# GpSimd adds the second layer norm's bias to each pair of expert tiles; the gates of the first stage are made at pair 8

## The chip, the cores and the metric

One of the eight cores of a Trainium2 chip runs the whole program. The metric is the device time of that core in microseconds (us). A run with a profile gives the span from the first to the last instruction, and its own time beside it.

## The reference

The input is x of 8 sequences with 256 tokens of 128 numbers, 2048 tokens, float32. Three residual steps follow each other: half of a mixture of experts, differential attention, and half of the same mixture again.

```
def ffn(x):                                   # per token, x is a layer-normed row
    p = softmax(x @ Wr + br)                  # 8 experts
    probs, idx = top_k(p, 2); probs /= probs.sum()
    h = layernorm(relu(x @ W1[e] + b1[e])) * g1[e] + be1[e]      # 128 -> 512
    y = layernorm(relu(h @ W2[e] + b2[e])) * g2[e] + be2[e]      # 512 -> 128
    return sum over the two chosen experts of gate[e] * y[e]
x = x + 0.5 * ffn(layernorm(x))
x = x + attention(layernorm(x))               # 8 heads, causal, lam = exp(lq1.lk1) - exp(lq2.lk2) + const
x = x + 0.5 * ffn(layernorm(x))
```

be2 is the bias that the change is about. Because it is added inside y[e], a token's output holds the sum of its two gates times its two rows of be2.

## The kernel before, in words

Only the two experts that a token chose are computed. The 4096 (token, expert) rows are sorted by expert into 39 tiles of 128 slots (`SLOT_TILES`), and the tiles go through the experts in 20 pairs (`PAIRS`); a tile has one expert, whose number each engine reads from the tile `eid` into a register (`experts`, L58). There are three stages: "f1" (first mixture), "at" (attention) and "f2" (second mixture). The order of the work on each engine is written out by hand, and semaphores join the engines.

**A pair in f1.** GpSimd gathers the rows of the pair's tiles from DRAM with an indirect DMA for each tile (`gather`, L517; `gather_pair(p)`, L535, fetches the tiles of pair p + 4 as soon as TensorE has turned those of pair p + 2). TensorE turns the rows (`turn_x`, L969), makes the hidden layer (`hidden`, L980), turns it (`turn_h`, L989) and makes the second product (`second`, L999). ScalarE empties PSUM (`copy_xT` L751, `relu` L758, `copy_hT` L764), makes square roots (L768, L772) and the last scaling (`finish`, L779), which writes the tile `yo` and counts the semaphore `yf`. VectorE makes the statistics (L1388 to L1419), adds the shifted bias b2 (L1407) and multiplies by g2 (`y_norm`, L1431). SyncE stores `yo` to the DRAM tensor y_scratch (L381) and, after every second pair, empties a part of another one (L428). In `body(n)` TensorE does turn_h(n), turn_x(n + 2), hidden(n + 1), second(n).

**Pairs 0 and 1** are written out, pairs 2 to 7 are a loop, and pairs 8 to 19 (`BESIDE` is 8) have work of the stages behind them woven in, by the functions `between(m)` and `behind(m)` of each engine with m = n - 8. For m = 0 to 3 TensorE and VectorE add the bias be2; from m = 3 on the y rows of sequences 0 and 1 are weighed and summed (`early_combine`, L2099) and their attention begins: statistics (L2109 to L2117), the root on GpSimd (`root`, L563), the norm (L2122). The y rows come by GpSimd's gathers (`token_rows`, L583), which wait for the stores of the pairs that they read.

**The bias be2 in f1.** The gates of the two choices are made ahead of pair 0: ScalarE takes the exponent of the logits' difference (L819), VectorE makes the gates (`gate_pairs`, L1271) and spreads them to a table of 8 experts for each token (`gate_sums`, L1277); TensorE turns this table (`turn_gates`, L1052), ScalarE copies it (L826). ScalarE also spreads be2 into the tile `be2x` with 16 copies (`own_bias`, L723). Four products of 128x512 (`shared_bias`, L1115) then give gates times be2 for all tokens, in pairs 8 to 11, and VectorE adds them to x (`add_bias`, L1459). The second mixture does the same at its end, with the same `be2x`. Beside the gates ScalarE and VectorE make lambda of the attention (L821, L1212, L1213).

**Around it.** `center_weights` (L2398) on VectorE comes behind the gates. On GpSimd `bias_rows` (L587) makes three rows from the router's bias for the second mixture, behind the last gather of f1. The attention (`att_gpsimd`, `att_scalar`, `att_tensor`, `att_vector`) begins with GpSimd's gathers of the y rows of sequences 2 and 3 (L1638), which wait for all y stores, and then runs in turns t = 2 to 9; each turn has on ScalarE `turned_half` (L945), the exponents (L1736), and `half_values` (L1715).

Of the kernel before, what the change touches and what calls it, by code (L numbers as in the profile page):

```python
# [21 lines left out]
P = 128  # L22
# [86 lines left out]
def build(nc, x, Wq, Wk, Wv, Wo, lq1, lk1, lq2, lk2, Wr, br, W1, b1, g1, be1, W2, b2, g2, be2, out, stages=("f1", "at", "f2")):  # L109
    with ExitStack() as ctx:  # L110
# [37 lines left out]
        be2x = sb("be2x", [P, TT, DIM])  # L148
        gmix = sb("gmix", [P, TOPK, TT, NE])
# [221 lines left out]
        def moe_sync(sp, S, first):  # L371
# [95 lines left out]
        def moe_gpsimd(pool, S, first):  # L467
# [71 lines left out]

            for p in range(BESIDE + 2):  # L540
                gather_pair(p)
            pool.wait_ge(S["gsum"], 1)
# [9 lines left out]
            gather_pair(BESIDE + 5)  # L552
            gather_rows(pool, 1, (1,))
            gather_pair(BESIDE + 6)
            gather_pair(BESIDE + 7)
            root(pool, 1)
            pool.tensor_scalar(picks[:, 0, 0, :], lo_iota[:, 0:NE], float(TT), None, ALU.mult).then_inc(F["base"], 1)
# [226 lines left out]
        def moe_scalar(act, S, first):  # L784
# [3 lines left out]
            if first:  # L788
# [39 lines left out]
            if first:  # L828
                gates_turned()
# [47 lines left out]
            if first:  # L877
# [127 lines left out]
        def moe_tensor(pe, S, first):  # L1005
# [50 lines left out]
            if first:  # L1056
                turn_gates()
# [17 lines left out]
            def between(m):  # L1075

                if m < 4:
                    shared_bias(m)
                if m == 4:
                    pe.wait_ge(s_ld_a, 80)  # L1080
                    pe.wait_ge(S["be2a"], 4)
                    turn_weights(pe, BESIDE_BANK)
# [28 lines left out]
            def shared_bias(q):  # L1111
                if first and q:
                    pe.wait_ge(S["be2a"], q)
                at = BESIDE_BANK if first else bank[BE2_BANKS[q]][:]
# [7 lines left out]
            if first:  # L1122
                turn_x(0, 0, 0)
                own_products(0)
                e = experts(pe, eid, 0, 6)
                pe.wait_ge(s_colc, 2 + NE)
# [310 lines left out]
        def expert_loop_vector(dve, S, step, first, steps):  # L1437
# [24 lines left out]
            def between(m):  # L1462

                if m < 4:
                    add_bias(m)
# [1097 lines left out]
```

## Time and profile before

| | us |
|---|---|
| runs of the kernel | 440.73, 441.86, 444.21 (median 441.86) |
| profiled execution, its own time | 438.17 |
| its span | 436.2 |
| TensorE busy | 385.0 |
| VectorE busy | 349.7 |
| ScalarE busy | 289.7 |
| GpSimd busy | 246.5 |

PE is TensorE's matmul, PEld its weight load, DVE is VectorE, ACT ScalarE, POOL GpSimd, SP SyncE. Times inside the profile count from the start of the span. A row of a timeline has start, duration, engine, line, operation and tiles; in brackets stands how long the engine was idle before it and what let it go. "issue" is time in which an engine waited for nothing that the profile shows. Matmuls overlap, so in the chain of waits a product counts 0.86 us where the timeline has 1.02 for the two of it.

### The profile page before, as it was taken

How to read it: one execution, taken by the hardware profiler on the slowest of the kernel's cores; microseconds unless marked ns; L12 is line 12 of the kernel's file. 1: busy time of each engine (PE TensorE's matmuls, PEld its weight loads, DVE VectorE, ACT ScalarE, POOL GpSimd, SP SyncE). 2: the span in 40 equal slices, each digit the busy share in tenths (PEclk: the TensorE clock that was granted, in tenths of full speed). 3: DMA queues.
4: the chain of work that ended last, by engine and by line, in shares of the span. 5: the costliest groups of instructions: out<-in, count | busy, mean ns of one | idle time of the engine just before them, and what ended most of it. 6: DMA issues, size and time to landing. Idle time of an engine off the chain costs nothing.

```text
span 436.2 us, 11622 instructions
## 1 busy us (share of the span) xinstructions
PE 385.0 (88%) x3570; PEld 271.8 (62%) x3574; DVE 349.7 (80%) x1302; ACT 289.7 (66%) x595; POOL 246.5 (57%) x343
## 2 busy tenths in 40 slices
PE   7887999999999868889898899887899899999864
PEld 7643577877777554556465565654577588787623
DVE  8895678887989797787888898867598788878864
ACT  3196787655777787778676778765665476776630
POOL 8786554346462056567574847568615767655530
PEclk9997999999999969999999999999999899999997
DMA  6930014654345311001000001011121222111036
GB/s 194 329 141 25 26 50 152 206 177 157 118 144 181 106 38 30 23 14 26 20 20 22 14 26 32 20 38 50 51 51 38 75 62 63 57 55 43 32 104 216
DMA packets 27444, 35.15 MB, mean 81 GB/s; under 512 B 4329, under 2 KB 20641, under 8 KB 26242
## 3 DMA queue, kind: packets, MB, share of 16 engines
q1 hardware_dynamic: 22450, 24.62, 17.3%
q0 software_dynamic: 4944, 9.90, 8.3%
q8 instruction: 27, 0.44, 0.4%
q14 instruction: 23, 0.19, 0.1%
HBM read 15.45 MB, written 18.24 MB: 77 GB/s over the span
## 4 chain that ended last, share of the span: by engine, by line
PE 50%; DVE 16%; POOL 12%; issue 8%; DMA 7%; ACT 4%; SPq 1%; DVEq 0%; POOLq 0%; ACTq 0%
PE bank L980 12%; PE bank L999 12%; PE bank L989 6%; DVE mx L2162 4%; POOL xr_scratch L463 3%; POOL orr L1669 2%; PE bank L1188 2%; DMA early<-y_scratch 2%; POOL yk L583 2%; DMA yk<-y_scratch,posi 2%; PE bank L969 2%; PE bank L2525 1%; PE bank L1925 1%; PE bank L1943 1%; PE bank L1183 1%
## 5 line engine op out<-in xcount | busy, mean ns | idle before, releaser
L999 PEld LDWEIGHTS bank<-w2c,hT 128*128 128x128 f32 x624 | 76.3, 194 | 21.8 <-issue 20.8
L999 PE MATMUL bank<-w2c,hT 128*128 x624 | 78.0, 279 | 3.5 <-ACT hT L764 3.4
L980 PE MATMUL bank<-w1s,xT 128*128 x156 | 74.1, 596 | 0.1
L2162 DVE TENSOR_REDUCE mx<-bank 128x4 f32<-128x1024 f32 (+1 forms) x48 | 58.4, 1220 | 8.6 <-PE bank L1885 8.6
L1736 ACT ACTIVATE early<-bank 128x768 f32<-128x768 f32 x64 | 51.8, 813 | 20.2 <-PE bank L1933 19.5
L1388 DVE BATCH_NORM_STATS2 st<-wide 128x6 f32<-128x512 f32 x78 | 50.0, 682 | 15.2 <-ACT wide L758 15.1
L764 ACT COPY hT<-bank 128x1024 f32<-128x1024 f32 (+1 forms) x40 | 39.5, 989 | 33.6 <-PE bank L989 33.6
L517 POOL DMA_INDIRECT xgw<-xn_scratch,slot_u x39 | 37.4, 958 | 34.1 <-PE bank L969 25.1
L487 POOL DMA_INDIRECT y_scratch<-yo,dest_u x39 | 38.9, 999 | 30.4 <-PE bank L989 16.0
L583 POOL DMA_INDIRECT yk<-y_scratch,posi x32 | 32.4, 1013 | 36.4 <-DMA y_scratch<-yo 14.4
L758 ACT ACTIVATE wide<-bank 128x1024 f32<-128x1024 f32 (+1 forms) x40 | 40.1, 1002 | 11.9 <-PE bank L980 11.1
L463 POOL DMA_INDIRECT xr_scratch<-row_buf,hi_i x32 | 31.8, 994 | 22.6 <-PE bank L1933 12.9
L989 PE MATMUL bank<-ident,wide 128*128 128x128 f32 x312 | 40.8, 273 | 0.0
L980 PEld LDWEIGHTS bank<-w1s,xT 128*128 128x128 f32 x156 | 27.0, 190 | 21.3 <-issue 21.0
L989 PEld LDWEIGHTS bank<-ident,wide 128*128 128x128 f32 x312 | 35.4, 142 | 0.8 <-issue 0.3
L945 ACT COPY wide<-bank 128x1024 bf16<-128x1024 bf16 x28 | 28.4, 1015 | 2.1 <-PE bank L1188 2.0
L1407 DVE SCALAR_TENSOR_TENSOR yy<-bank,r,b2p 128x128 f32<-128x128 f32 x78 | 24.6, 351 | 6.1 <-DVE r L1401 1.6
L779 ACT ACTIVATE yo<-yz,r 128x128 f32<-128x128 f32 x78 | 27.1, 397 | 3.3 <-DVE yz L1431 2.1
L1925 PE MATMUL bank<-mxT,sel 64*128 64x384 bf16 x128 | 21.5, 333 | 6.4 <-ACT early L1736 4.1
L1876 PE MATMUL bank<-mrhs,mlhs 64*128 64x128 bf16 (+1 forms) x192 | 15.6, 242 | 12.0 <-DVE mx L2162 9.2
L1431 DVE SCALAR_TENSOR_TENSOR yz<-yy,mv,g2b 128x128 f32<-128x128 f32 x78 | 23.4, 339 | 0.0
L563 POOL TENSOR_TENSOR ars<-ave,neg_half 128x2 f32<-128x2 f32 x8 | 5.8, 719 | 29.6 <-DVE ave L2117 29.6
(382 smaller groups left out, 880.2 us busy)
## 6 DMA issues: line engine op xcount, KB each, us to landing
xr_scratch<-row_buf SPq DMA_DIRECT2D x8, 1032.0 KB
xgw<-xr_scratch SPq DMA_DIRECT2D x39, 64.5 KB, 1.8
y_scratch<-yo SPq DMA_DIRECT2D x19, 128.0 KB, 1.9
w1s<-in_L_ffn_W_dram SPq DMA_DIRECT2D x1, 2048.0 KB, 8.9
early<-y_scratch SPq DMA_DIRECT2D x8, 256.0 KB, 4.0
xs<-in_L_attn_x_dram SPq DMA_DIRECT2D x4, 256.0 KB, 3.8
xn_scratch<-row_buf SPq DMA_DIRECT2D x1, 1024.0 KB
out_dram<-xs SPq DMA_DIRECT2D x8, 128.0 KB, 2.4
```

Of the source, the lines that this page charges most:

```text
L463: pool.indirect_dma_start(out=xr_dram, out_offset=bass.IndirectOffsetOnAxis(ap=slot2[:, c:c + 1], axis=0), in_=rows_of[t // HALF][:, t % H ...
L487: pool.indirect_dma_start(out=y_dram, out_offset=bass.IndirectOffsetOnAxis(ap=dest_u[:, 2 * p + j:2 * p + j + 1], axis=0), in_=yo[:, p % 2 ...
L517: pool.indirect_dma_start(out=xg[:, u, :], out_offset=None, in_=xn_dram, in_offset=bass.IndirectOffsetOnAxis(ap=slot_u[:, n:n + 1], axis=0 ...
L583: pool.indirect_dma_start(out=yk4[:, t % (2 * YRING), k, :], out_offset=None, in_=done, in_offset=bass.IndirectOffsetOnAxis(ap=posi[:, c:c ...
L758: act.activation(hh[:, u, 0:k, :], banks[:, h_at[u]:h_at[u] + k, :], ACT.Relu).then_inc(S["relu"], 1)
L764: act.copy(hT[:, u, 0:k, :], banks[:, 5:5 + k, :]).then_inc(S["hTc"], 1)
L980: last = pe.matmul(bank[h_at[u] + j][:], xT[:, u, j, :], w1s[:, bass.ds(e * FF, FF)], start=True, stop=True)
L989: last = pe.transpose(bank[5 + j][:, c * P:c * P + P], hh[:, u, j, c * P:(c + 1) * P], ident[:])
L999: last = pe.matmul(o[:, j * DIM:(j + 1) * DIM], hT[:, u, j, c * P:(c + 1) * P], w2c[:, bass.ds(e * (FC * DIM) + c * DIM, DIM)], start=(c = ...
L1388: last = dve.bn_stats(st1[:, u, j, :], hh[:, u, j, :])
L1736: act.activation(prob[:, g], quad[:, low:low + 2, 0:3 * P], ACT.Exp).then_inc(A["prob"], 1)
L2162: dve.tensor_reduce(mx[:, c:c + 2 * per].rearrange("p (a q) -> p q a", q=2), quad[:, low:low + 2, :].rearrange("p q (a e) -> p q a e", a=p ...
```

## The change

GpSimd adds be2 of the tile's expert to each row of `yo`, right behind ScalarE's last scaling, from a tile `be2b` that holds be2 of all experts on all partitions (loaded by one more broadcast DMA of 512 KB; it lies in the first half of `be2x`). SyncE's store waits for GpSimd's add (semaphore `be2`) in place of `yf`. With that, the first mixture's four bias products, their additions, the table of gate sums, its turn and its copy are gone. Both exponents become powers of e on GpSimd, behind the first gathers; VectorE makes the gates and lambda in pair 8. The adds stand one pair of gathers behind: `after_gather(p)` adds to pair p - 2. `bias_rows` and the second root come later in GpSimd's order. ScalarE's 16 copies into `be2x` move to the ends of the attention's turns 2 to 5, four each.

```diff
+        be2b = be2x[:].rearrange("p t d -> p (t d)")[:, 0:NE * DIM]
@@ moe_sync
-                    sp.wait_ge(S["yf"], p + 1)
+                    sp.wait_ge(S["be2"], p + 1)
@@ moe_gpsimd
+            def add_rows(p, es):
+
+                pool.wait_ge(S["yf"], p + 1)
+                for j in tiles[p]:
+                    last = pool.tensor_tensor(yo[:, p % 2, j, :], yo[:, p % 2, j, :], be2b[:, bass.ds(es[j] * DIM, DIM)], ALU.add)
+                last.then_inc(S["be2"], 1)
+
+            def after_gather(p):
+
+                at = (p - 2) % 4
+                if at == 0:
+                    after_gather.es = experts(pool, eid, 2 * p - 4, min(PACK, SLOT_TILES - 2 * p + 4))
+                add_rows(p - 2, after_gather.es[2 * at:])
+
+            pool.wait_ge(S["eid"], 1)
+            pool.wait_ge(s_bc, 32)
             for p in range(BESIDE + 2):
                 gather_pair(p)
+                if p == 0:
+                    pool.wait_ge(S["top"], 1)
+                    pool.tensor_tensor(gden[:], euler[:], mw[:], ALU.pow).then_inc(S["gexp"], 1)
+                if p == 1:
+                    pool.wait_ge(A["lam"], 1)
+                    pool.tensor_tensor(lam_e[:], euler[:, 0:2], lam_s[:], ALU.pow).then_inc(A["lame"], 1)
+                if p >= 2:
+                    after_gather(p)
             pool.wait_ge(S["gsum"], 1)
             pool.wait_ge(S["yst0"], 8 * BESIDE)
             pool.wait_ge(S["yst1"], 8 * BESIDE)
             gather_rows(pool, 0, (0,))
             gather_pair(BESIDE + 2)
+            after_gather(BESIDE + 2)
             gather_rows(pool, 0, (1,))
             gather_pair(BESIDE + 3)
+            after_gather(BESIDE + 3)
             root(pool, 0)
             gather_pair(BESIDE + 4)
+            after_gather(BESIDE + 4)
...
             gather_pair(BESIDE + 7)
+            after_gather(BESIDE + 7)
+            pool.tensor_scalar(picks[:, 0, 0, :], lo_iota[:, 0:NE], float(TT), None, ALU.mult).then_inc(F["base"], 1)
+            after_gather(BESIDE + 8)
             root(pool, 1)
-            pool.tensor_scalar(picks[:, 0, 0, :], lo_iota[:, 0:NE], float(TT), None, ALU.mult).then_inc(F["base"], 1)
+            for p in range(BESIDE + 9, PAIRS + 2):
+                after_gather(p)
             bias_rows(pool)
@@ moe_scalar, ahead of pair 0, and in pairs 0 and 1
-                act.wait_ge(S["top"], 1)
-                act.activation(gden[:], mw[:], ACT.Exp).then_inc(S["gexp"], 1)
-                act.wait_ge(A["lam"], 1)
-                act.activation(lam_e[:], lam_s[:], ACT.Exp).then_inc(A["lame"], 1)
-                act.activation(spad, eps_c[:], ACT.Sqrt)
-            if first:
-                gates_turned()
-                own_bias(act, 0, 4)
-                own_bias(act, 4, 10)
-                own_bias(act, 10, 16)
@@ moe_tensor
-            if first:
-                turn_gates()
-                if m < 4:
-                    shared_bias(m)
-                pe.wait_ge(S["gTc"], 1)
-            pe.wait_ge(s_be2x, 3)
@@ moe_vector and expert_loop_vector
-                gates(dve, S, step)
-                dve.wait_ge(A["lame"], 1)
-                step(dve.tensor_tensor(neg_lam[:], lam_e[:, 1:2], lam_e[:, 0:1], ALU.subtract))
-                step(dve.tensor_scalar(neg_lam[:], neg_lam[:], -LAMBDA_INIT, None, ALU.add))
             def between(m):
-                if m < 4:
-                    add_bias(m)
+                if m == 0:
+                    gate_pairs(dve, S, step)
+                    lambda_difference(dve, step)
+                    dve.memset(hold[:, 0:1], 0.0).then_inc(S["gsum"], 1)
@@ att_scalar, the end of a turn
+                if t == 2:
+                    act.wait_ge(sems["f1"]["be2"], PAIRS)
+                if 2 <= t < 2 + TT // BIAS_STEP:
+                    own_bias(act, BIAS_STEP * (t - 2), BIAS_STEP * (t - 1))
@@ center_weights and the prologue of gpsimd
-            dve.wait_ge(s_bc, 16)
+            dve.wait_ge(s_bc, 32)
+            pool.dma_start(be2b, be2.rearrange("(o a) d -> o (a d)", o=1).to_broadcast([P, NE * DIM])).then_inc(s_bc, 16)
```

`BIAS_STEP` is 4. TensorE's wait for the finished W1 (`s_colc`) moves ahead of the turn of pair 0.

## Rows read from the trace of the kernel before

**Rows 1.** The page, busy time of each engine, us and share of the span.
```profile
PE 385.0 (88%) x3570; PEld 271.8 (62%) x3574; DVE 349.7 (80%) x1302; ACT 289.7 (66%) x595; POOL 246.5 (57%) x343
```
**Rows 2.** Busy time by stretch; columns: stretch, length, PE, PEld, DVE, ACT, POOL, clock, DMA, GB/s.
```profile
58.60:81.80 23.20, 23.20 (x153) 18.17 (x152) 19.09 (x86) 17.63 (x40) 9.51 (x11) 1.00 0.44 150
...
86.40:108.20 21.80, 21.80 (x130) 16.06 (x129) 17.40 (x73) 13.06 (x28) 11.60 (x12) 1.00 0.49 163
108.20:129.60 21.40, 20.55 (x132) 15.91 (x132) 18.72 (x86) 15.57 (x38) 11.31 (x12) 1.00 0.43 139
129.60:149.00 19.40, 17.28 (x133) 13.64 (x132) 17.42 (x82) 15.04 (x32) 3.49 (x13) 1.00 0.40 137
```
**Rows 3.** Timeline ahead of pair 0, all engines.
```profile
38.30 0.97 POOL L517 DMA_INDIRECT xgw<-xn_scratch,slot_u  x1 [0.30 <-issue]
...
39.59 1.02 PE L2416 MATMUL bank<-early,yz 128*32 128x512 f32 x2
39.84 1.28 ACT L819 ACT_TABLE_LOAD   x1
...
43.47 0.38 PE L969 MATMUL bank<-ident,xgw 128*128 128x128 f32 x2
```
**Rows 4.** Row gathers (L517) from 36 to 50 us.
```profile
DMA to landing us min/median/max: 2.5/2.6/2.8
```
**Rows 5.** GpSimd's timeline in pairs 9 to 17.
```profile
93.40 0.94 POOL L517 DMA_INDIRECT xgw<-xn_scratch,slot_u  x1 [3.24 <-PE bank L969]
...
97.23 0.94 POOL L583 DMA_INDIRECT yk<-y_scratch,posi  x1 [1.64 <-DMA y_scratch<-yo]
...
113.75 0.74 POOL L563 TENSOR_TENSOR ars<-ave,neg_half 128x2 f32<-128x2 f32 x1 [6.59 <-DVE ave L2117]
...
138.12 0.71 POOL L563 TENSOR_TENSOR ars<-ave,neg_half 128x2 f32<-128x2 f32 x1 [8.46 <-DVE ave L2117]
...
142.26 0.20 POOL L599 TENSOR_TENSOR picked<-picked 128x8 bf16<-128x8 bf16 x1
```
**Rows 6.** The chain of waits in pairs 8 to 17; columns: start, duration, what.
```profile
87.68 0.86 PE bank L1115 x2
...
127.37 4.41 DMA xgw<-xn_scratch,slot_u
...
132.22 1.98 PE bank L980 x4
```
**Rows 7.** GpSimd's groups by shape; after the bar: busy us, mean ns.
```profile
L1633 POOL TENSOR_SCALAR row_buf<-xs,mv,rstd 128x128 f32<-128x128 f32 x12 | 10.1, 849 | 0.7
...
L1613 POOL TENSOR_TENSOR ysum<-yk 128x256 f32<-128x256 f32 x5 | 3.6, 715 | 0.0
...
L510 POOL TENSOR_TENSOR gden<-euler,mw 128x16 f32<-128x16 f32 x1 | 2.9, 2942 | 0.0
...
L2487 POOL DMA_DIRECT2D g2b<-in_L_ffn_g_dram x1 | 0.5, 533 | 0.0
...
L2363 POOL TENSOR_TENSOR b1lo<-early,b1hi 32x128 f32<-32x128 f32 x1 | 0.4, 421 | 0.1
```
**Rows 8.** Timeline behind the last pair.
```profile
152.47 0.40 ACT L779 ACTIVATE yo<-yz,r 128x128 f32<-128x128 f32 x1
...
155.26 1.32 POOL L583 DMA_INDIRECT yk<-y_scratch,posi  x1 [12.80 <-DMA y_scratch<-yo]
...
162.22 1.14 DVE L2099 SCALAR_TENSOR_TENSOR xs<-yk,gate,xs 128x128 f32<-128x128 f32 x4 [0.23 <-DMA yk<-y_scratch,posi]
```
**Rows 9.** ScalarE's spread of the bias, its first call.
```profile
49.80 1.27 ACT L725 ACTIVATE be2x<-be2p,own_t 128x128 f32<-128x128 f32 x4
```
**Rows 10.** ScalarE's timeline at the end of the attention's turn 2.
```profile
177.42 1.01 ACT L945 COPY wide<-bank 128x1024 bf16<-128x1024 bf16 x1
178.94 0.59 ACT L1715 COPY turned_o<-bank 128x512 f32<-128x512 f32 x1 [0.51 <-PE bank L1947]
```
**Rows 11.** VectorE's addition L2193, eight times; ns min/median/max.
```profile
L2193 DVE TENSOR_TENSOR od<-ow x8: 416/453/1298, 184.2 to 316.8; 128x256 f32<-128x256 f32 x8
```

More of the change, by code:

```diff
@@ L546, in moe_gpsimd @@
             gather_pair(BESIDE + 2)
+            after_gather(BESIDE + 2)
             gather_rows(pool, 0, (1,))
             gather_pair(BESIDE + 3)
+            after_gather(BESIDE + 3)
             root(pool, 0)
             gather_pair(BESIDE + 4)
+            after_gather(BESIDE + 4)
             gather_rows(pool, 1, (0,))
             gather_pair(BESIDE + 5)
+            after_gather(BESIDE + 5)
             gather_rows(pool, 1, (1,))
             gather_pair(BESIDE + 6)
+            after_gather(BESIDE + 6)
             gather_pair(BESIDE + 7)
+            after_gather(BESIDE + 7)
+            pool.tensor_scalar(picks[:, 0, 0, :], lo_iota[:, 0:NE], float(TT), None, ALU.mult).then_inc(F["base"], 1)
+            after_gather(BESIDE + 8)
             root(pool, 1)
-            pool.tensor_scalar(picks[:, 0, 0, :], lo_iota[:, 0:NE], float(TT), None, ALU.mult).then_inc(F["base"], 1)
+            for p in range(BESIDE + 9, PAIRS + 2):
+                after_gather(p)
             bias_rows(pool)
@@ L1111, in shared_bias @@
             def shared_bias(q):
-                if first and q:
-                    pe.wait_ge(S["be2a"], q)
-                at = BESIDE_BANK if first else bank[BE2_BANKS[q]][:]
+                at = bank[BE2_BANKS[q]][:]
                 pe.matmul(at, gsT[:], be2x[:, 4 * q:4 * q + 4, :], start=True, stop=True).then_inc(S["be2"], 1)
@@ L1122, in moe_tensor @@
             if first:
+                pe.wait_ge(s_colc, 2 + NE)
                 turn_x(0, 0, 0)
@@ L1125, in moe_tensor @@
                 e = experts(pe, eid, 0, 6)
-                pe.wait_ge(s_colc, 2 + NE)
                 hidden(0, 0, e[0:2])
@@ L1152, in moe_tensor @@
                 return
+            pe.wait_ge(s_be2x, TT // BIAS_STEP)
             e = experts(pe, eid, 2 * PAIRS - 8, 7)
@@ L1165, in build @@
         BE2_BANKS = (0, 1, 2, 4)
+        BIAS_STEP = 4
         def turn_weights(pe, at):
@@ L1265, in tiles_used, with lambda_difference @@
             step(dve.tensor_scalar(first_at[:], tile_iota[0:1, 0:40], used[:, 0:1], float(P), ALU.add, ALU.mult))
-        def gates(dve, S, step):
-            gate_pairs(dve, S, step)
-            gate_sums(dve, S, step)
+        def lambda_difference(dve, step):
+            dve.wait_ge(A["lame"], 1)
+            step(dve.tensor_tensor(neg_lam[:], lam_e[:, 1:2], lam_e[:, 0:1], ALU.subtract))
+            step(dve.tensor_scalar(neg_lam[:], neg_lam[:], -LAMBDA_INIT, None, ALU.add))
         def gate_pairs(dve, S, step):
@@ L1458, in add_bias @@
                 x4 = xs[:, 4 * q:4 * q + 4, :]
-                dve.tensor_tensor(x4, x4, (BESIDE_BANK if first else bank[BE2_BANKS[q]][:]).rearrange("p (t d) -> p t d", t=4), ALU.add
+                dve.tensor_tensor(x4, x4, bank[BE2_BANKS[q]][:].rearrange("p (t d) -> p t d", t=4), ALU.add
                                   ).then_inc(S["be2a"], 1)
             def between(m):
-                if m < 4:
-                    add_bias(m)
+                if m == 0:
+                    gate_pairs(dve, S, step)
+                    lambda_difference(dve, step)
+                    dve.memset(hold[:, 0:1], 0.0).then_inc(S["gsum"], 1)
                 if m == 4:
@@ L1481, in behind @@
                 if m == 3:
-                    dve.wait_ge(S["be2a"], 4)
                     steps["early_combine"](0, 0)
```

1 line of the change is left out of this document (removed).

## The prediction

> **What bounds the kernel now.** I read the page first: it names TensorE as the busiest engine, 88% of the span [rows 1]. But an average does not say what one stage is worth, so I went to the table by stretches, then to the chain of waits of the stretches that the change touches, and to GpSimd's timeline. In the steady loop TensorE has no gap at all, 23.20 of 23.20 us for five pairs (4.64 us a pair), while VectorE has 19.09 and GpSimd 9.51 [rows 2]. Pairs 8 to 11 take 21.80 us, 5.45 each, again without a gap. Pairs 12 to 15 take 21.40 us and TensorE has gaps.
>
> Ahead of the loop the chain runs through the gates: ScalarE loads the table for Exp at 39.84, VectorE makes the gates and their sums, TensorE turns them and only then, at 43.47, starts pair 0 [rows 3]. In pairs 14 to 16 the chain leaves TensorE and goes down GpSimd's queue of gathers of x rows and y rows: the last gather for pair 18 goes out at 127.37 and lands 4.41 us later, and TensorE's hidden product of pair 17 starts at 132.22 [rows 6]. What holds GpSimd back there is first the root, which waits 6.59 us for VectorE's variance [rows 5]. Behind the loop the chain is: last y store, GpSimd's gathers of the y rows of tokens of sequence 2, VectorE's sum [rows 8]. A measurement of this kernel tells about 1%, 4.4 us, from no change.
>
> **Ahead of the loop.** Gone from the path are the Exp table load and two Exps, three steps of gates, two products, the sum, two steps of lambda and the turn on TensorE. What is late next is the row gather for pair 0: its second tile is issued at 38.30 [rows 3] and gathers of this stretch land 2.6 us after issue (median) [rows 4], so at 40.9; TensorE's weight sums end at 40.6 [rows 3]. The prologue has one more broadcast DMA; an issue of this kind costs GpSimd 0.53 us [rows 7]. The first gather was let go by VectorE, not by this prologue, so some of it is hidden, and I add 0.3 to 0.5. Pair 0's turn then starts at 41.2 to 41.4 in place of 43.47: 2.1 us sooner. Bounds: 1.5 (all of it late, and the landing slower) to 2.6 (nothing late). All later steps of the start hang on it. The copies that made the spread bias on ScalarE (four take 1.27 us, [rows 9]) stand in front of the copies of hT, but TensorE is in the hidden product of the next pair meanwhile, so they give nothing more, 0 to 0.4 us. The extra 512 KB come in beside the weights, more than 10 us ahead of their readers; the page has some 300 GB/s in that slice, so they hold the others up by 1.7 us at most, and the one who needs W2 then, ScalarE, still waits for TensorE afterwards: nothing, with 0 to 0.5 kept for the range.
>
> **Pairs 0 to 7.** TensorE stays the bound, 4.64 us a pair. GpSimd gets the power for the gates: 2.94 us (the same form, 128x16, is in the second expert stage), the small one 0.7 [rows 7]. Both stand between gathers that are issued two pairs ahead, and GpSimd is idle over half of each pair [rows 2], so by my count it has caught up by pair 4 and no gather is late. An add of 128x128 on GpSimd does not occur before. Nearest rows: an add-like one of 32x128, as many elements a partition on fewer partitions, in 0.42 us, 128x256 in 0.715, and the dearest 128x128 form, a two-step scalar one, 0.85 [rows 7]. I take 0.42 and 1.0 us for a pair with its waits and address registers; bounds 0.6 (two of the cheapest form, 0.20 for 128x8 [rows 5], and the gaps) and 1.9 (two of 0.85). A pair then costs GpSimd 2.2 of gathers, 0.3 of gap and 1.0, within 4.64. The store leaves 1 us later than it did; its buffer is wanted two pairs on, over 6 us later: nothing. VectorE has gate steps and lambda in pair 8, about 1.4 us in place of an add of 0.66, against an idle 0.8 us a pair and a bank that gives it one pair of slack: nothing.
>
> **Pairs 8 to 11.** Four bias products of 0.86 us leave TensorE's path (the chain's first row of [rows 6] is one): 3.45 us. With the start TensorE could be 5.5 us early at pair 12. **But GpSimd's queue becomes the bound.** I count it through. The gathers at 93.40 [rows 5] start at 93.40 - 2.1 - 0.86 = 90.4. From there to the last gather of pair 18 there are 19 issues ahead of it, 1.25 us apart (0.95 and a gap of 0.30): 23.75. Five pairs of adds at 1.0: 5.0. The store of pair 7 must land before the first y gather; that took 2.7 us from its end (94.55 to 97.23) and now starts when the add ends: 2.7 of idle time. The root: 0.9, and its wait of 6.59 is gone, since GpSimd comes there at 108.6, just when VectorE's variance does. The wait for landed y rows (1.6) is filled by an add. 90.4 + 23.75 + 5.0 + 2.7 + 0.9 + 0.1 = 122.85, where it was 127.37: **4.5 us sooner**, and TensorE is let go 4.5 us sooner, not 5.5 (plus the two gaps that it has now, 1.9 together). With 0.6 for a pair of adds it is 6.5, with 1.9 it is nothing.
>
> **Pairs 16 to 19 and the tail.** GpSimd had 8.5 us of idle time there; the adds fit. The last add comes behind the last finish (ends 152.87): 0.42 and 0.15 of wait before the store may go. Worse, the router's bias rows, which GpSimd made from 139.2 to 142.5 while it was idle, now come behind the last add: 3.25 us, in the shade of a store that took 2.4 us from finish to first gather (155.26) [rows 8]. 0.6 + 3.25 + 0.25 - 2.4 = 1.7, and VectorE had 0.23 us of slack at the sum: **+1.6**. Bounds 0.6 (only the add) and 2.2.
>
> **Attention.** ScalarE makes the spread bias here, four copies (1.27 us) at the end of each of the turns 2 to 5. At that place it had 0.5 us before it was released by TensorE [rows 10]; so the copy of half the values is 0.7 us late, TensorE's turn of them too, and with it the next scores. The chain goes through these at the ends of turns 2 and 5; at 3 and 4 it goes through GpSimd's norm and combination, which hides it. 2 x 0.7 = **+1.4**; bounds 0 and 4 x 0.8 = 3.2.
>
> **Sum.** -4.5 + 1.6 + 1.4 = -1.5 us. The profiled execution (span 436.2, time 438.17) would come to 436.7. The median of the runs, 441.86, is 3.7 above the profiled one, and I keep that: 440.4.
>
> **The rule that speaks against it.** VectorE's addition with two inputs in SBUF takes 453 ns in the median and 1298 at worst (L2193) [rows 11]; the long ones lie beside element work of GpSimd. The Trainium skill, "GPSIMD Engine Reference", section "Key points", says that GpSimd shares its SBUF interfaces with VectorE and contends with two-input instructions and two-port modes. The trace agrees with that sentence. The Trainium skill, on the same page (section "Engine selection") calls a two-input elementwise op on GpSimd about twice as slow as on VectorE; by that the 0.35 us of a 128x128 op on VectorE would be 0.7, an estimate, and the sum would come to +1.6 us.
>
> **Rivals.**
> A: GpSimd is not the bound (adds of 0.3 us, or landings of 2.6 and not 4.4 us). For: its queue is a third idle. Against: the count above. TensorE keeps 5.5 and loses its gaps of 1.9: -7.4 + 1.6 + 1.4 = -4.4: 437.5.
> B, slower: the adds are dear. A pair with its register loads takes 1.9 us, as the dearest 128x128 row would give; GpSimd's queue then gives back all of the 4.5, the tail has 0.4 more: +3.4, 445.3. It turns at 1.3 us a pair, where 4.5 is down to 3.0. For: the address comes from a register, which no GpSimd row shows. Against: the rows of 128 and 256 elements fit one line.
> C: contention. If each pair of adds held VectorE for its 0.84 us, the loop would just reach its bound (3.82 + 0.84 = 4.66), and pairs 12 to 19, where VectorE is busy 36.1 of 40.8 us [rows 2], would have 42.8 us of work: 42.8 without a gap, 48.4 with gaps as now, 45.8 between. Against the forecast's 41.8 that is 4 more: +2.5, 444.4. Against: most of VectorE's time in a pair is statistics, which read one input.
> That the change doesn't do what it says I exclude: each removed instruction stands in the trace.
>
> **Chances.** Forecast 0.5 (its own range 438.5 to 442.5), A 0.22, B 0.15, C 0.08, 0.05 for the rest. Range 436.0 to 445.0: A and most of B. Faster by over 1% (under 437.4): half of A and a little of the forecast's tail and the scatter of medians, 0.23; slower by over 1% (over 446.3): 0.10; within: 0.67.
>
> **What would show it.** Right: pair 0's turn at about 41.3; steps of 4.6 us in pairs 8 to 11; GpSimd without a long gap from 90 to 123 and TensorE waiting for a gather in pairs 13 to 16; the last gather of pair 18 at about 123; a gap of 1.7 us more between last finish and first y gather, with bias rows in it; half_values late by 0.7 us at the turns' ends. Wrong: adds over 0.6 us, a loop pair over 4.7, VectorE ops longer in the loop, or TensorE's wait in pair 15 or 16 gone.

## The result and the profile after

The changed kernel takes 444.50 us in the median of 20 runs (440.95 to 448.60), the kernel before, run beside it, 441.12 us (20 runs): a ratio of 1.0095, 95% interval 1.0067 to 1.0122. So it is slower by 1%, about 4 us, where I had forecast 1.5 us faster. Here and below a ratio and its interval come from the runs that are not over 1.5% above the fastest of their kernel, so a ratio is not that of the two medians beside it. The profiled execution has a span of 441.2 us against 436.2, 5.0 more; the comparison of the two traces has these 5.0 us to explain.

The page of the changed kernel, busy time of each engine in us:

```profile
PE 385.6 (87%) x3564; PEld 272.3 (62%) x3565; DVE 351.9 (80%) x1296; ACT 286.1 (65%) x589; POOL 267.8 (61%) x385
```

Against [rows 1], GpSimd has 21.3 us more. TensorE's busy time has not fallen, although four products of 0.86 us and the turn of the gates are gone. I read this as time that came back elsewhere, at a lower clock: the mean granted clock of this execution is 0.970 against 0.975.

**The loop did what was forecast.** The next fence is the timeline of the changed kernel around the start of pair 0, then of GpSimd alone through pairs 9 to 19; columns as in [rows 5].

```profile
41.31 0.33 PE L993 MATMUL bank<-ident,xgw 128*128 128x128 f32 x1 [0.74 <-DMA xgw<-xn_scratch,slot_u]
...
90.46 0.95 POOL L518 DMA_INDIRECT xgw<-xn_scratch,slot_u  x1 [1.49 <-PE bank L993]
...
92.69 0.87 POOL L545 TENSOR_TENSOR yo<-yo,be2x 128x128 f32<-128x128 f32 x2
96.19 0.95 POOL L617 DMA_INDIRECT yk<-y_scratch,posi  x1 [2.63 <-DMA y_scratch<-yo]
...
108.85 0.72 POOL L597 TENSOR_TENSOR ars<-ave,neg_half 128x2 f32<-128x2 f32 x1 [1.24 <-DVE ave L2136]
...
122.73 0.94 POOL L518 DMA_INDIRECT xgw<-xn_scratch,slot_u  x1 [0.30 <-issue]
...
135.34 0.73 POOL L597 TENSOR_TENSOR ars<-ave,neg_half 128x2 f32<-128x2 f32 x1 [5.35 <-DVE ave L2136]
```

Pair 0's second tile is turned at 41.31 (forecast 41.2 to 41.4), the gathers of pair 13 are issued at 90.46 (90.4), a pair of adds takes 0.87 to 0.94 us and about 1.0 with its gaps (1.0), the root waits 1.24 us instead of 6.59, and the last gather of pair 18 goes out at 122.73 (122.85), 4.6 us sooner than the 127.37 of [rows 6]. What I had not counted comes right behind it. From 125.15 on VectorE works with no idle time worth a row until 143.38, and the rest of the loop is its own:

```profile
125.15 1.17 DVE L2118 SCALAR_TENSOR_TENSOR xs<-yk,gate,xs 128x128 f32<-128x128 f32 x2 [2.44 <-DMA yk<-y_scratch,posi]
...
143.38 0.63 DVE L1421 SCALAR_TENSOR_TENSOR yy<-bank,r,b2p 128x128 f32<-128x128 f32 x2 [0.19 <-issue]
```

(Of the rows between these two none has idle time before it.) So the last finish ends at 149.17 instead of 152.87: 3.7 us are gained by then, 0.8 less than forecast.

**The gain is lost behind the loop.** GpSimd and VectorE behind the last pair:

```profile
149.47 0.45 POOL L545 TENSOR_TENSOR yo<-yo,be2x 128x128 f32<-128x128 f32 x1 [1.36 <-ACT yo L813]
149.87 0.38 POOL L625 CAST picked<-brb 128x8 bf16<-128x8 f32 x1
...
153.28 0.20 POOL L633 TENSOR_TENSOR picked<-picked 128x8 bf16<-128x8 bf16 x1
...
154.06 1.08 POOL L617 DMA_INDIRECT yk<-y_scratch,posi  x1 [0.57 <-POOL picked L633]
```
```profile
161.14 1.14 DVE L2118 SCALAR_TENSOR_TENSOR xs<-yk,gate,xs 128x128 f32<-128x128 f32 x4 [3.06 <-DMA yk<-y_scratch,posi]
```

The router's bias rows take the whole stretch from 149.87 to 153.48, and the first token gather issues 4.9 us behind the last finish, against 2.4 before [rows 8]. VectorE waits 3.06 us for the rows, where it waited 0.23. TensorE does its share of turn 2, which started 3.7 us sooner, and then has nothing: columns are stretch, length, busy us (instructions), granted clock, DMA share, GB/s.

```profile
158.00:162.00 4.00, 2.67 (x43) 0.92 0.20 53
162.00:164.00 2.00, 0.00 (x0) 1.00 0.12 33
164.00:166.00 2.00, 1.21 (x14) 0.86 0.00 0
166.00:168.00 2.00, 2.00 (x14) 0.50 0.25 66
168.00:170.00 2.00, 2.00 (x25) 0.79 0.14 33
208.00:210.00 2.00, 1.50 (x18) 0.95 0.00 0
210.00:212.00 2.00, 2.00 (x18) 0.50 0.00 0
212.00:214.00 2.00, 2.00 (x36) 0.69 0.03 8
```

It stands still for 3.29 us up to 164.79, and behind that its granted clock falls from 1.00 (2.4 GHz) to 0.50 (1.2 GHz). Here are the two projections of turn 2 in the chain of waits of the changed kernel, the first at the low clock, the second at the higher one again; then the ends of turns 2 to 5, where ScalarE's four spread copies now stand on the chain each time:

```profile
163.38 0.73 POOL ars L597
166.96 1.58 PE bank L1200 x2
169.59 0.84 PE bank L1200 x2
...
178.54 1.17 ACT be2x L759 x4
...
197.98 1.17 ACT be2x L759 x4
...
204.31 1.84 DVE od L2212
...
209.62 1.36 PE bank L1200 x2
...
220.54 1.17 ACT be2x L759 x4
...
241.76 1.17 ACT be2x L759 x4
```

A turn can be timed by ScalarE's copy of `mxT` near its start (162.51 and 180.95 before, 158.81 and 181.53 after, for turns 2 and 3). From one such copy to the next, in us (from ScalarE's timeline of each profiled execution):

| kernel | first at | turn 2 | 3 | 4 | 5 | 6 | 7 | 8 |
|---|---|---|---|---|---|---|---|---|
| before | 162.5 | 18.4 | 19.1 | 20.5 | 20.7 | 20.1 | 19.3 | 18.7 |
| changed | 158.8 | 22.7 | 19.4 | 22.6 | 21.2 | 19.5 | 19.3 | 20.3 |

Turn 2 takes 4.3 us more, turn 4 2.1 (its clock falls at 210), turn 8 1.6 (it falls at 292), and that is nearly all of what turned -3.7 into +5.0.

### The profile page after: what moved, and what is told of

It is laid out like the page before. It is cut to its first block, busy times and chain, and to the rows that moved or that the text cites. A ratio compares the mean times of both kernels' runs of the same rounds, so it can differ in the third digit from the quotient of the medians.

```text
span 441.2 us, 11762 instructions
## 1 busy us (share of the span) xinstructions
PE 385.6 (87%) x3564; PEld 272.3 (62%) x3565; DVE 351.9 (80%) x1296; ACT 286.1 (65%) x589; POOL 267.8 (61%) x385
## 4 chain that ended last, share of the span: by engine, by line
PE 41%; DVE 13%; POOL 12%; issue 10%; ACT 6%; DMA 6%; SPq 1%; DVEq 1%; POOLq 1%
PE bank L1004 9%; PE bank L1023 8%; PE bank L1013 5%; DVE mx L2181 3%; POOL xr_scratch L464 3%; POOL yk L617 3%; ACT wide L969 2%; POOL xgw L518 2%; PE bank L1944 2%; PE bank L1200 2%; DMA early<-y_scratch 2%; ACT early L1751 1%; PE bank L1895 1%; PE bank L993 1%; PE bank L2045 1%
## 5 line engine op out<-in xcount | busy, mean ns | idle before, releaser
L1023 PEld LDWEIGHTS bank<-w2c,hT 128*128 128x128 f32 x624 | 75.4, 192 | 21.4 <-issue 20.3
L1023 PE MATMUL bank<-w2c,hT 128*128 x624 | 76.6, 276 | 3.5 <-ACT hT L798 3.4
L518 POOL DMA_INDIRECT xgw<-xn_scratch,slot_u x39 | 37.4, 960 | 20.1 <-PE bank L993 10.4
L617 POOL DMA_INDIRECT yk<-y_scratch,posi x32 | 32.0, 1002 | 26.9 <-PE bank L1952 16.9
L1004 PEld LDWEIGHTS bank<-w1s,xT 128*128 128x128 f32 x156 | 26.6, 190 | 19.8 <-issue 19.5
L545 POOL TENSOR_TENSOR yo<-yo,be2x 128x128 f32<-128x128 f32 x39 | 17.3, 468 | 12.3 <-ACT yo L813 12.0
```

The lines of the kernel that those rows point to most:

```text
L518: pool.indirect_dma_start(out=xg[:, u, :], out_offset=None, in_=xn_dram, in_offset=bass.IndirectOffsetOnAxis(ap=slot_u[:, n:n + 1], axis=0 ...
L617: pool.indirect_dma_start(out=yk4[:, t % (2 * YRING), k, :], out_offset=None, in_=done, in_offset=bass.IndirectOffsetOnAxis(ap=posi[:, c:c ...
L1004: last = pe.matmul(bank[h_at[u] + j][:], xT[:, u, j, :], w1s[:, bass.ds(e * FF, FF)], start=True, stop=True)
L1023: last = pe.matmul(o[:, j * DIM:(j + 1) * DIM], hT[:, u, j, c * P:(c + 1) * P], w2c[:, bass.ds(e * (FC * DIM) + c * DIM, DIM)], start=(c = ...
```

## The experiments

The kernel before was run beside each group of four, so ratios are compared, not medians of different groups; e1 to e5 are one group, e6 to e9 the second, e10 to e13 the third. "Clock" is the median over the runs of the mean granted clock; the kernel before has 0.972, 0.971 and 0.970 in the three groups.

| run | median us | before us | ratio | 95% interval | clock |
|---|---|---|---|---|---|
| e1_rows_early | 438.32 | 439.11 | 0.9960 | 0.9923 to 0.9998 | 0.972 |
| e2_copies_late | 443.49 | 439.11 | 1.0097 | 1.0059 to 1.0134 | 0.960 |
| e3_both | 438.84 | 439.11 | 0.9976 | 0.9944 to 1.0008 | 0.969 |
| e5_before_copies | 441.64 | 439.11 | 1.0018 | 0.9982 to 1.0053 | 0.974 |
| e6_copies_hidden | 435.23 | 440.58 | 0.9906 | 0.9874 to 0.9938 | 0.974 |
| e7_before_rows_late | 441.97 | 440.58 | 1.0048 | 1.0012 to 1.0083 | 0.968 |
| e8_warm | 440.69 | 440.58 | 1.0014 | 0.9979 to 1.0049 | 0.969 |
| e9_no_adds | 435.95 | 440.58 | 0.9924 | 0.9888 to 0.9961 | 0.970 |
| e10_changed_again | 442.36 | 440.48 | 1.0068 | 1.0035 to 1.0100 | 0.966 |
| e11_copies_hidden_only | 440.64 | 440.48 | 1.0017 | 0.9980 to 1.0053 | 0.964 |
| e12_warm_start | 434.79 | 440.48 | 0.9903 | 0.9868 to 0.9938 | 0.980 |
| e13_best_again | 436.22 | 440.48 | 0.9932 | 0.9896 to 0.9968 | 0.972 |

**Bias rows early.**
```diff
             root(pool, 1)
+            bias_rows(pool)
             for p in range(BESIDE + 9, PAIRS + 2):
                 after_gather(p)
-            bias_rows(pool)
```

> The changed kernel, with bias_rows called right behind root(1) (where GpSimd idles 5 us in the trace of the changed kernel, ahead of the adds of pair 15) instead of behind the last add. Nothing else differs. Theory 1 (the tail: bias_rows' 3.6 us from 149.87 to 153.48 stand ahead of the first token gather at 154.06 and delay all that hangs on the gathers): the first token gather issues about 3.6 us sooner after the last add, and TensorE does not stand still at 162 to 164 us and keeps a granted clock near 1.00 at 166 to 170 us; together about 3 us less than the changed kernel, so about 1 us above the kernel before. Theory 2 (the 16 spread copies of ScalarE alone make the loss; the gathers have slack): the same as the changed kernel within 0.5 us, about 4 us above the kernel before.

Theory 1 holds, and its 3 us were too few: the ratio goes from 1.0095 to 0.9960, 1.35% or 6 us (from 1.0068 of the repetition below, 4.8 us), and clock and time are those of the kernel before. GpSimd's timeline behind the last add in this run, and TensorE's stretches of turn 2:

```profile
148.75 0.46 POOL L545 TENSOR_TENSOR yo<-yo,be2x 128x128 f32<-128x128 f32 x1 [1.36 <-ACT yo L813]
151.51 1.08 POOL L617 DMA_INDIRECT yk<-y_scratch,posi  x1 [2.30 <-issue]
```
```profile
162.00:164.00 2.00, 1.85 (x24) 1.00 0.12 33
164.00:166.00 2.00, 1.98 (x25) 1.00 0.21 66
166.00:168.00 2.00, 2.00 (x43) 1.00 0.00 0
```

The gather now issues 2.3 us behind the add (what is left is the store), not 4.1 as in the changed kernel. It is 1.8 us, not the 3.6 of the bias rows, since half of them had lain in the shade of the store. But turn 2 takes 18.9 us instead of 22.7: 3.8 less. One delay of 1.8 us costs twice its size. The other 2 us are in the two traces as well. From the issue of the fourth y gather to VectorE's sum it is 2.5 us here and 3.2 in the changed kernel, which makes 0.7. From the root of sequence 2 to turn 3 it is 16.9 us here and 18.1 in the changed kernel, which makes 1.2; there the clock was at 0.50.

**Spread copies late, and both.**
```diff
-                if t == 2:
-                    act.wait_ge(sems["f1"]["be2"], PAIRS)
-                if 2 <= t < 2 + TT // BIAS_STEP:
-                    own_bias(act, BIAS_STEP * (t - 2), BIAS_STEP * (t - 1))
...
+                if t >= BATCH:
+                    own_bias(act, BIAS_STEP * (t - BATCH), BIAS_STEP * (t - BATCH + 1))
                 if D_:
                     outputs_turned(d)
```
(with `BIAS_STEP = 8`)

> The changed kernel, with ScalarE's 16 spread copies of the bias not four each at the ends of turns 2 to 5 but eight each in turns 8 and 9, ahead of the turned outputs, where ScalarE idles over 2 us in the trace of the changed kernel. Theory 1 (each group of four stands on the chain of waits, 1.17 us at each of four turn ends, against my forecast of two turn ends at 0.7): 4 x 1.17 = 4.7 us less than the changed kernel, about 0.5 us below the kernel before. Theory 2 (my forecast: two ends at 0.7): 1.4 us less, about 2.8 us above the kernel before. Theory 3 (the loss is the low granted clock at 164 to 170, 208 to 214 and 290 to 296 us, which follows stretches of idle TensorE): under 1 us less, with the clock still at 0.50 in these stretches.

> Both edits together: bias_rows right behind root(1) and the 16 spread copies in turns 8 and 9. If tail and copies are separate terms, the gains add: 3 + 4.7 = 7.7 us below the changed kernel, about 3.5 us below the kernel before (what is left is the 4.5 us gained in the loop less the last add of 0.5 us and the shifted end). If they share one cause (a late second turn that leaves TensorE idle and its clock low), the sum is less than the sum of the two: about 5 us below the changed kernel.

Neither gained anything: 1.0097 against 1.0095, and 0.9976 against 0.9960. By the totals I would have said that the copies cost nothing. The turns say otherwise: without copies turns 3 to 5 of the run with both edits take 19.1, 20.4 and 20.7 us, as before, but turn 8, which got eight of them, takes 22.0 instead of 18.7. Part of these 3.3 us is a stretch at 0.50 in the same turn (294 to 300 us): in profiles that have such a stretch in turn 8 and no copies there, the turn takes 20.1 to 20.3. So about half of it is left for the copies. I had moved the cost: the idle time that I had seen there lay in turn 9, not in turn 8. What it did show is turn 2 without copies but with late bias rows: 23.2 us, with the same fall of the clock (0.50 at 164 to 168 us). So turn 2's loss is not the copies'.

**The two parts put into the kernel before.**
```diff
@@ att_scalar, the end of a turn (first run)
+                if 2 <= t < 6:
+                    own_bias(act, 4 * (t - 2), 4 * (t - 1))
@@ moe_gpsimd (second run)
+            pool.wait_ge(S["yf"], PAIRS)
             bias_rows(pool)
```

> The kernel before, with the 16 spread copies made a second time, four each at the ends of turns 2 to 5, where the changed kernel has them (the same values are written again, so the output is unchanged). Theory 1 (each group of four is on the chain): 4 x 1.17 = 4.7 us above the kernel before. Theory 2 (my forecast): 1.4 us above it. Theory 3 (the copies are hidden in the rhythm of the kernel before and cost only in the shifted rhythm of the changed one): within 0.5 us of the kernel before.

> The kernel before, with one wait added: bias_rows waits for the last rows of the loop, so that its 3.6 us stand between the last finish (152.9 us) and the first token gather, as in the changed kernel. Theory 1 (this place alone makes the loss): the first token gather issues at 157.1 instead of 155.3, 1.9 us late, and TensorE runs dry in turn 2: 1.9 us above the kernel before by the delay alone, and 3 to 4 us above it if the clock falls as well. Theory 2 (the loss needs the adds and the copies of the changed kernel): within 0.5 us of the kernel before.

With the copies, turns 2 to 5 take 1.1, 0.3, 0.6 and 0.5 us more than in the kernel before, turn 6 takes 0.6 less: 1.9 in all, of which 0.6 is a later landing of the y rows in turn 2, ahead of all copies. It is near my forecast of 1.4 and far from 4.7, though the copies stand on the chain at three of the four ends (179.31, 219.76, 241.01). Standing on the chain is not the same as costing one's length: what they push off must have had a wait of its own to give (this is my reading; no run tests it). The profile has a fall of the clock in turn 8 besides, +1.6; the ratio of 1.0018 has room for 0.8 us less or 2.3 more.

With the bias rows late, the first gather is at 157.6 instead of 155.3, turn 2 takes 21.2 us instead of 18.4, and TensorE has the same picture, idle (2.2 us without a break) and then a clock that is at its low level for most of 4 us:

```profile
166.00:168.00 2.00, 0.32 (x2) 1.00 0.04 12
168.00:170.00 2.00, 2.00 (x25) 0.57 0.12 33
170.00:172.00 2.00, 2.00 (x14) 0.57 0.21 66
```

The whole is 1.0048 times the kernel before, 2.1 us (0.5 to 3.7): the order of GpSimd's queue costs by itself, in a kernel that has neither adds nor copies. It costs less here than in the changed kernel: VectorE waits 1.7 us longer for the rows than in the kernel before, where the changed kernel waits 2.8 longer; the clock takes the same 1.2 us in both.

**TensorE kept busy in turn 2.**
```diff
                     if A_ and g == 1:
+                        for _ in range(14 if t == 2 else 0):
+                            pe.matmul(bank[7][:], ones16[:], iota_rep[:, 0:64, :].rearrange("p a b -> p (a b)"), start=True, stop=True)
                         turn_norm(pe, t, bank[7])
```

> The changed kernel, with 14 matmuls of 128x512 whose result nobody reads put ahead of the transposes of turn 2, where TensorE stands still for 3.3 us (161.5 to 164.8 us in the trace of the changed kernel). Bias_rows stays behind the last add. Theory 1 (part of the loss of turn 2 is the granted clock, which falls to 0.50 at 166 to 168 us behind this gap): the clock stays at 1.00 there, the two projections take 0.84 us instead of 1.58, and turn 3 starts 1.2 to 1.6 us sooner; whole time 1.5 us less, 443 us where the changed kernel has 444.5, or 3 us less if later falls of the clock go as well. Theory 2 (the clock has no part in it; the turn waits for GpSimd and DMA): the same time as the changed kernel, or up to 0.5 us more.

```profile
162.00:164.00 2.00, 2.00 (x11) 1.00 0.12 33
164.00:166.00 2.00, 1.28 (x8) 1.00 0.00 0
166.00:168.00 2.00, 1.85 (x24) 1.00 0.14 33
```

The clock stays at 1.00, and in the chain the two projections take 0.84 us each. The whole comes to 1.0014 against 1.0095 and 1.0068 for the changed kernel: 0.5 to 0.8%, 2.4 to 3.6 us, for matmuls that compute nothing. The kernels stand in different groups, and the interval touches that of the repetition (0.9979 to 1.0049 against 1.0035 to 1.0100), so the size is loose. Theory 1 holds for the clock and the projections; the whole is nearer to the larger of its two figures. The time from the root of sequence 2 (`ars`) to turn 3's `mxT` copy prices the fall in turn 2 by itself. It is 16.4 to 16.6 us in the profiles with neither copies nor fall (before, and those with both places mended), 16.9 with copies (e1, e8), 18.1 in the changed kernel, 18.1 in e2, which has the fall and no copies, 17.7 in e7 and 18.6 in e11, which have no copies there either. So the fall costs 1.2 us in turn 2 in the changed kernel and in e7, 1.6 in e2 and 2.1 in e11, and the copies 0.5. The rest of the gain came in later turns (turn 4 takes 21.1 us and turn 8 18.7, without a fall), but turn 5 had one.

**The adds left out.**
```diff
-                for j in tiles[p]:
-                    last = pool.tensor_tensor(yo[:, p % 2, j, :], yo[:, p % 2, j, :], be2b[:, bass.ds(es[j] * DIM, DIM)], ALU.add)
-                last.then_inc(S["be2"], 1)
+                pool.tensor_copy(yo[0:1, p % 2, 0, 0:1], yo[0:1, p % 2, 0, 0:1]).then_inc(S["be2"], 1)
```

> The changed kernel with bias_rows right behind root(1) and without the 39 adds: GpSimd touches one element of each pair's rows instead of adding the bias, so the first half's output lacks this bias; reads of the expert numbers, waits and semaphores stay. Theory 1 (my forecast: in pairs 8 to 17 GpSimd's queue sets the loop, so each add of 0.9 us a pair is paid there): 10 x 0.8 = up to 8 us less than with the adds, but not more than TensorE's own bound allows; the last finish of the loop then ends at 141 to 146 us instead of 148.5, and the whole time is 433 to 436 us. Theory 2 (GpSimd's queue has slack, TensorE sets the pairs): the last finish ends within 0.5 us of 148.5 and the whole time is within 0.7 us of 438.3.

The last finish ends at 145.87, 2.6 us sooner than with the adds (148.45 in e1), and the ratio is 0.9924 against 0.9960. So the adds did bound a part of the loop, as forecast, but they cost 2.6, not 8. GpSimd is busy for 23.00 of the 36 us from 90 on, with the adds for 26.60 (e1):

```profile
90.00:126.00 36.00, 23.00 (x30) 1.00 0.51 156
```

Leaving out the adds takes two things away: time in GpSimd's queue, and a neighbour of VectorE's operations. The traces tell them apart. Here are VectorE's sum, GpSimd's root behind it, and VectorE's last sum that waits for rows, without the adds and then in e1, with them:

```profile
106.55 0.58 DVE L2116 SCALAR_TENSOR_TENSOR xs<-yk,gate,xs 128x128 f32<-128x128 f32 x2
108.22 0.73 POOL L595 TENSOR_TENSOR ars<-ave,neg_half 128x2 f32<-128x2 f32 x1 [2.34 <-DVE ave L2134]
122.32 0.61 DVE L2116 SCALAR_TENSOR_TENSOR xs<-yk,gate,xs 128x128 f32<-128x128 f32 x2 [0.31 <-DMA yk<-y_scratch,posi]
```
```profile
106.41 1.22 DVE L2118 SCALAR_TENSOR_TENSOR xs<-yk,gate,xs 128x128 f32<-128x128 f32 x2
108.72 0.72 POOL L597 TENSOR_TENSOR ars<-ave,neg_half 128x2 f32<-128x2 f32 x1 [1.25 <-DVE ave L2136]
124.76 0.81 DVE L2118 SCALAR_TENSOR_TENSOR xs<-yk,gate,xs 128x128 f32<-128x128 f32 x2 [2.17 <-DMA yk<-y_scratch,posi]
```

GpSimd waits at the root in both, so the adds ahead of it are free, and this is why 2.6 us come out and not 8. With the adds the root is 0.5 us later, because the sum beside an add (106.53 to 107.47) takes 1.22 us instead of 0.58. From the root to the last sum the gap grows to 2.4: the 1.9 us between are two pairs of adds in GpSimd's queue, for which VectorE then waits. Behind that sum only 0.14 us are added.

**The copies hidden, and the square closed.**
```diff
                 body(0, 0, lag=0)
+                own_bias(act, 8, 12)
                 body(1, 1, lag=1)
+                own_bias(act, 12, 16)
@@ the second loop's start
             sqrt1(1, 1)
+            act.wait_ge(sems["f1"]["be2"], PAIRS)
+            own_bias(act, 0, 8)
             turned_batch(act, F, d)
```
(and nothing in the turns; `bias_rows` early, but for e11)

> The changed kernel with bias_rows right behind root(1), and with the 16 spread copies moved out of the attention turns: those of tiles 8 to 15, whose half of be2x the rows of the bias do not use, behind ScalarE's part of pairs 0 and 1, where it idles 1.3 to 1.5 us in the trace of the changed kernel; those of tiles 0 to 7 in the second loop ahead of the last batch of routing, where it idles 2.6 us. Compared with the run that moved bias_rows alone (438.32 us median; its four turns with copies are 0.3 to 1.0 us longer each than the turns of the kernel before): if the copies' place costs, 2 us less, 436.3 us. If the copies cost only where TensorE's clock falls anyway: the same within 0.5 us, 438.3 us. If the copies behind pairs 0 and 1 stand on the path of the loop: 439.5 us.

> The changed kernel as it is, once more, so that it stands beside the other three of this call on one chip. 3 to 5 us above the kernel before, mean granted clock 0.96 against 0.97 before. If its first result had been a matter of that chip, it comes out within 1 us of the kernel before.

> The changed kernel with the 16 spread copies behind pairs 0 and 1 and in the second loop, as in the run before, but with bias_rows left behind the last add: the fourth corner of the square. With both places mended the time was 5.4 us below the kernel before; with bias_rows alone mended 0.8 us below it. If the two terms add: the copies' term of 3 to 4 us comes off the changed kernel here too, so 0 to 1 us above the kernel before. If the copies cost only once the gathers are early enough (they share the slack of turn 2): 3 to 4 us above the kernel before, as the changed kernel.

> The version with both places mended once more, on the chip of the three others: 4 to 6 us below the kernel before (ratio 0.987 to 0.991), and 8 to 9 us below the changed kernel. If its first result had been luck of the clock, it comes out at most 2 us below the kernel before.

This version beats both kernels: 0.9906 and, on another chip, 0.9932 times the kernel before (3 to 4 us less by the ratios, 4.3 to 5.4 by the medians). The repetition is less than I had expected of it (0.987 to 0.991): the first result had some luck. The square, ratios to the kernel before:

| | copies in turns 2 to 5 | copies hidden |
|---|---|---|
| bias rows behind the last add | 1.0095, 1.0068 | 1.0017 |
| bias rows early | 0.9960 | 0.9906, 0.9932 |

The place of the bias rows is worth 0.9% with the copies hidden (both in one group: 4.4 us between the medians) and 1.1 to 1.4% without; the place of the copies 0.5 to 0.8% with late rows (1.7 us between the medians of one group) and 0.3 to 0.5% with early ones. The terms add within the intervals, and the rows are the larger. The smallest of these differences, 0.3%, is within the intervals of its two ratios. Repeated, the changed kernel came out 3.0 us above the kernel before by the ratio (1.9 by the medians) and not 4; its interval overlaps the first one's and leaves out 1. Turn 2's low clock is in all five profiles with late bias rows and nothing to fill the gap (changed, e2, e7, e10, e11), where TensorE had stood still for 2.2 to 3.9 us just before, and in none of the nine others, where this gap is 0.3 to 1.3 us long. The profiled execution of the repetition is the slowest of its runs (446.01) and shows the mechanism at its worst: root to turn 3 takes 20.4 us, with

```profile
162.00:164.00 2.00, 0.00 (x0) 1.00 0.13 33
164.00:166.00 2.00, 0.39 (x2) 0.80 0.00 0
166.00:168.00 2.00, 2.00 (x24) 0.50 0.11 33
168.00:170.00 2.00, 2.00 (x10) 0.50 0.24 66
170.00:172.00 2.00, 2.00 (x23) 0.50 0.00 0
```

**TensorE kept busy ahead of turn 2.** The kernel before and the changed one both have a low clock at some 152 to 162 us. Four unused matmuls follow each of five groups of scores:
```diff
+                for n in range(1, 6):
+                    batch_scores(0, n, False)
+                    for _ in range(4):
+                        pe.matmul(bank[0][:], ones16[:], iota_rep[:, 0:64, :].rearrange("p a b -> p (a b)"), start=True, stop=True)
```

> The version with both places mended, with four matmuls of 128x512 whose result nobody reads behind each of the five groups of scores ahead of turn 2, where TensorE idles 0.3 to 2.1 us at a time and its granted clock falls to 0.50 at 152 to 160 us, in this version as in the kernel before. Theory 1 (turn 3 hangs on the first token gather at 152.2 us by way of the root and the projections, so a faster TensorE ahead of turn 2 only waits): the clock stays near 1.00, turn 2 starts up to 1 us sooner, turn 3 starts at the same time within 0.3 us, and the whole time is within 0.7 us of that version. Theory 2 (the low clock there is on the path): 1 to 2 us less.

The clock stays at 1.00 from 40 to 338 us, and turn 3 starts at 176.0 in this run as in e13 (turn 2 starts 0.5 us later, not sooner): the low clock ahead of turn 2 is hidden behind the gathers, and the same clock 10 us later is not. The whole is 1.4 us less than e13 by medians; the intervals overlap almost wholly, so whether anything is gained is open.

## Why the prediction was wrong

By its own steps:

- **Ahead of the loop**, 2.1 us: right (41.31).
- **Pairs 8 to 11 and GpSimd's queue**, 4.5 us: right at the place it was counted for (4.6). At the last finish 3.7 is left in the first profile; over the profiles of the changed order with its adds this end lies at 147.8 to 149.4, against 152.9 to 153.2 with the old order, so 3.5 to 5.3. What I missed is that VectorE sets pairs 17 to 19. Rival A (GpSimd not the bound) falls by the run without adds, though only for the part behind the root (about 1.9 us of the 2.6).
- **The adds**: 460 ns each in the median, 0.87 to 0.94 a pair, which is what I took. Rival B (1.9 a pair) falls. The Trainium skill, "GPSIMD Engine Reference", section "Engine selection", has a two-input operation on GpSimd at about twice VectorE's time, from which I had worked out 0.7 us; the measured 0.46 decides, which is 1.3 times the 0.35 us of VectorE's 128x128 operations.
- **Rival C**, contention in the loop: it is there, at a small price. VectorE has 19.52 us of work in five pairs with the adds against 19.09 [rows 2], 0.1 a pair, and pairs 0 to 7 keep their pace. From 60 to 148 us the eight sums `xs` take 544 ns in the mean instead of 344, which was one of my signs of being wrong; by the run without adds 0.5 to 0.6 us of this reach the last finish, not the 4 us that I gave it. In the attention the addition `od` took 1.92 us in turn 4 and 2.02 in turn 5 beside GpSimd's product of 128x512; before the change the longest of its eight took 1298 ns [rows 11]. All eight together take 7.0 to 7.1 us in each of the six profiles with copies in turns 2 to 5, and 4.6 to 6.4 in the eight others (4.6 before). So a part of what the copies cost may be this contention; what it adds to the time was not tested.
- **The tail**, +1.6: **this is the step that failed.** I said that bias_rows come "behind the last add", "in the shade of a store", and took what sticks out of the shade. That part was low but not far off: 2.5 us (4.9 against 2.4) between last finish and first gather. I then let it cost its own length, and my sum has no term for TensorE's clock. The place of these rows costs 0.9 to 1.4%, 4 to 6 us (the square), of which the traces show 3.8 in turn 2: 1.8 for the gathers, 0.7 for rows that landed later than in e1, and 1.2 for the clock. Turn 2 had been brought forward by the loop's gain and its rows of sequence 2 had not, so TensorE ran dry for 3.3 us, and behind this gap its clock was 0.50. The bounds that I gave, 0.6 to 2.2, came from the delay alone. [rows 8] had the warning: VectorE had 0.23 us of slack at the sum, so from there on each late gather was on the path.
- **Attention**, +1.4: the size is near by the run on the kernel before (1.9 from the turns) and rather low by the square (1 to 3), the places wrong: I had them hidden at the ends of turns 3 and 4, and they show at all four. What they cost above that goes with falls of the clock. Among the profiles with copies in turns 2 to 5, the changed kernel, its repetition, e1, e8 and e9 have a stretch at 0.50 in turn 3, 4 or 5, and only e5 has none; without copies there, e11 alone of eight has one (before, e2, e3, e6, e7, e12 and e13 have none); e2 and e3, whose copies lie in turns 8 and 9, have one in turn 8. That is how often it was seen, one profile each; that the copies bring it about was not tested apart.

In sum, -3.7 at the last finish; +2.6 up to the root, nearly all for the gathers; +0.4 copies and +1.2 clock in turn 2, which makes turn 3 0.6 late; +0.4 and +2.1 in turns 3 and 4; +0.5, -0.6 and 0 in turns 5 to 7; +1.6 in turn 8 and +0.5 behind it: 5.0, but for rounding. The times of single runs follow the clock: over 35 runs of the kernel before a mean clock lower by 0.01 goes with 3.2 us more in each of two groups (correlation -0.80 and -0.86), with 2.3 over 33 runs in the third (-0.67). Without the runs over 1.5% above the fastest it is 3.0, 2.5 and 1.4 us (-0.79, -0.73 and -0.50). The changed kernel's median clock is 0.959. So the profile's own share of falls is partly luck, and the medians carry the verdict.

Why the clock falls in turn 8 of some executions (the changed kernel's and its repetition's, e1, e5, e6, e9, e11, and e2 and e3 with copies there) and not of others (before, e7, e8, e12, e13) stays open. It costs about 1.6 us and was not provoked or prevented by itself.

## What to carry to other kernels

When work is moved along an in-order queue to a place "behind the last" of something, look at what is next in that queue, not only at how long the moved work is: ten tiny instructions, 3.6 us long, stood ahead of gathers with 0.2 us of slack, while the same queue had idled 5 us a little earlier. A gain ahead of such a point is only kept if what the next stage waits for is brought forward as well; otherwise the fast engine runs dry, and in the five profiles here where it did, it paid for the gap once more, by the granted clock behind it. And judge a moved cost by the stages it left and entered: the totals of the second and third run said "free" where the turns said "moved".

## What was not expected of the hardware

- 14 matmuls without a use, put into one gap of 3.3 us, made the changed kernel 0.5 to 0.8% faster. TensorE's granted clock stayed at 1.00 (2.4 GHz) behind them, which is worth 1.2 us in turn 2; the rest came in later turns.
- A small operation on GpSimd that reads the rows of an expert through a register's address shows no extra price: 448 to 526 ns for 128x128 (39 times), between the 421 ns of 32x128 and the 715 ns of 128x256 with fixed addresses [rows 7]; no 128x128 add with a fixed address was run. Its address registers take 46 to 51 ns:

```profile
L545 POOLq FUSED_REGOPS  x39: 46/46/51, 59.4 to 149.3; - x39
L545 POOL TENSOR_TENSOR yo<-yo,be2x x39: 448/460/526, 63.0 to 149.5; 128x128 f32<-128x128 f32 x39
```

- The same y gathers land later in some profiles. From the issue of the fourth, which VectorE's sum waits for, to the sum's start it took 3.2 to 3.8 us in the five profiles of the changed kernel with late bias rows (157.95 to 161.14 in the changed kernel) and 2.4 to 2.5 in the six with early ones (155.40 to 157.89 in e1). On the kernel before it was 2.8, with late rows 2.5 and with the copies 3.4, so the place of the rows alone does not explain it; the reason stays open.
- Beside GpSimd's adds some of VectorE's operations are longer: between 60 and 148 us the sums of 128x128 took 475 to 565 ns in the mean in the ten profiles with adds, and 340 to 345 in the four without (before, e5, e7, e9).
